# Attention loop with merges ahead of maxima, spread gate values, an earlier output weight and a moved transposition

## The reference, cut to what matters

```
mod = silu(c) @ wmod;  ga = sign(ga) * max(|ga|, 0.25)
h = layernorm(x) * (1 + ca) + sa
x = x + ga * (softmax(mask(q k^T / 4)) v) @ wo          # block 0, attention
h = layernorm(x) * (1 + cb) + sb
gate = softmax over the 16 best of 64 experts
x = x + gb * ((h @ A.T) * gate) @ B.T * 2               # block 0, mixture
w1 = (Wq + Wk + Wv + low rank parts) / 3                # block 1, decoded from 4-bit codes
```

## Time and profile before

| | us |
|---|---|
| median of 3 runs | 947.92 |
| lowest, highest | 945.81, 948.16 |
| profiled execution, its own time | 945.97 |
| span of its instructions | 944.2 |
| PE busy | 861.7 (91%) |
| DVE busy | 681.2 (72%) |
| ACT busy | 533.1 (56%) |
| POOL busy | 191.1 (20%) |
| mean granted TensorE clock | 0.974 of 2.4 GHz |

### The profile page before, as it was taken

The page is one execution under the profiler, slowest core; times in us unless marked ns, Lnnn a source line. Parts: engine busy times, 40 slices in busy tenths (PEclk is TensorE's granted clock), DMA queues, the critical chain, the costliest instruction groups (busy, mean ns, idle before and its releaser), DMA issues.

```text
span 944.2 us, 13669 instructions
## 1 busy us (share of the span) xinstructions
PE 861.7 (91%) x5096; PEld 679.8 (72%) x5096; DVE 681.2 (72%) x1066; ACT 533.1 (56%) x707; POOL 191.1 (20%) x199
## 2 busy tenths in 40 slices
PE   3799899998859699998999999999988999999996
PEld 1466666666637587786888888788876888888885
DVE  3845777888769677688777778577787866667842
ACT  3412576667652525476566667477727766666830
POOL 3002565677637114200000000000040000000004
PEclk9798899999989999999999999999989999999999
DMA  8587378878534112115233333143312433332202
GB/s 297 177 254 158 35 99 130 126 91 129 89 90 167 34 45 73 51 33 161 81 107 110 105 96 89 46 111 90 114 43 68 115 107 90 110 92 67 67 1 90
DMA packets 38450, 95.35 MB, mean 101 GB/s; under 512 B 7144, under 2 KB 10216, under 8 KB 37360
## 3 DMA queue, kind: packets, MB, share of 16 engines
q1 hardware_dynamic: 34256, 89.11, 38.9%
q10 hardware_dynamic: 4128, 5.36, 1.7%
HBM read 79.56 MB, written 2.21 MB: 87 GB/s over the span
## 4 chain that ended last, share of the span: by engine, by line
PE 59%; DVE 6%; issue 2%; ACT 2%; POOL 1%; DMA 1%; SPq 0%; POOLq 0%; DVEq 0%; ACTq 0%
PE PS L1602 13%; PE PS L1603 13%; PE PS L1604 13%; PE PS L1913 5%; PE PS L1912 5%; PE PS L1911 5%; POOL X L776 1%; DVE ACC L1224 1%; PE PS L1894 1%; DVE SCR L1209 1%; PE PS L1882 1%; PE PS L1646 1%; DVE ST L1151 1%; DMA WOF<-in_WO 1%; PE PS L1841 1%
## 5 line engine op out<-in xcount | busy, mean ns | idle before, releaser
L899 ACT ACTIVATE PL<-CODE 128x1024 f32<-128x1024 int32 x200 | 202.5, 1057 | 58.8 <-DVE ACC L1224 56.1
L1602 PE MATMUL PS<-HH,WRH 128*128 128x512 f32 x448 | 177.0, 395 | 9.8 <-DVE WRL L1236 4.4
L1603 PE MATMUL PS<-HH,WRL 128*128 128x512 f32 x448 | 176.3, 393 | 0.0
L1604 PE MATMUL PS<-HL,WRH 128*128 128x512 f32 x448 | 176.0, 393 | 0.0
L776 POOL TENSOR_TENSOR X<-X,SCR 128x512 f32<-128x512 f32 x32 | 42.5, 1339 | 560.7 <-DVE SCR L1209 560.6
L1224 DVE SCALAR_TENSOR_TENSOR ACC<-PL,ACC 128x1024 f32<-128x1024 f32 x100 | 122.8, 1228 | 8.4
L947 ACT ACTIVATE PT<-PS 128x512 f32<-128x512 f32 x160 | 85.4, 601 | 57.9 <-PE PS L1720 38.5
L793 POOL TENSOR_TENSOR QS<-ident,MX 64x256 fp32r<-64x256 f32 x128 | 97.2, 759 | 71.9 <-DVE MX L1381 51.6
L1602 PEld LDWEIGHTS PS<-HH,WRH 128*128 128x128 f32 x448 | 85.2, 190 | 29.8 <-issue 5.4
L1604 PEld LDWEIGHTS PS<-HL,WRH 128*128 128x128 f32 x448 | 85.2, 190 | 17.9
L1603 PEld LDWEIGHTS PS<-HH,WRL 128*128 128x128 f32 x448 | 85.1, 190 | 17.2
(11 more groups left out here) (230 smaller groups left out, 1525.2 us busy)
## 6 DMA issues: line engine op xcount, KB each, us to landing
CODE<-in_CODES SPq DMA_DIRECT2D x50, 512.0 KB, 3.5
SCALE<-in_SCALES SPq DMA_DIRECT2D x100, 256.0 KB, 4.0
WM<-in_WM SPq DMA_DIRECT2D x12, 1024.0 KB, 5.3
QS<-FQ SPq DMA_DIRECT2D x32, 256.0 KB, 5.2
X<-in_X ACTq DMA_DIRECT2D x2, 1024.0 KB, 12.7
KS<-KHL SPq DMA_DIRECT2D x32, 64.0 KB, 5.3
KN<-KHL SPq DMA_DIRECT2D x32, 64.0 KB, 4.2
GAB<-gates SPq DMA_DIRECT2D x4, 512.0 KB, 3.7
```

What stands on the lines that cost most here:

```text
L899: nc.scalar.activation(PL[:, n % 3], CODE[:, p % 2], ACT.Prelu, scale=scale, bias=bias, alpha=alpha).then_inc(s_plane, 1)
L1602: nc.tensor.matmul(dst, lh, rh, start=start and k == 0, stop=False)
L1603: nc.tensor.matmul(dst, ll, rh, start=False, stop=False)
L1604: ins = nc.tensor.matmul(dst, lh, rl, start=False, stop=stop and k == KC - 1)
```

## The change

- `step_at` loses its shift by one slot: every decoding step is one slot earlier, and the last fold lies in the loop, behind unit 62's exponentials on ACT. Three entries of `CODES_AT` and `SCALES_AT` move one stack ahead to match it.
- `add_odd_values` stands ahead of the maxima of unit 12, 20, ..., 60, and `add_odd_sums` behind the maxima of the same unit.
- The four operations of the gate values lie behind units 2, 5, 6 and 10. SP stores the gates at stack 6, not 3.
- SP waits for the last curve (`s_plane`), not for the last sum, ahead of the load of `WOF`. ACT rounds `WOF` after the exponentials of unit 63.
- `a1` is transposed after the sixth output product, and DVE copies it ahead of the seventh gated output.

```
-CODES_AT = {0: (0, 1), 4: (2,), 6: (3,), 9: (4,), 12: (5,)}
-SCALES_AT = {0: (0, 1), 6: (2,), 9: (3,), 13: (4,), 15: (5,)}
+CODES_AT = {0: (0, 1), 4: (2,), 6: (3,), 9: (4,), 11: (5,)}
+SCALES_AT = {0: (0, 1), 6: (2,), 8: (3,), 12: (4,), 15: (5,)}
+A1_AT = 5
+GATE_AT = [2, 5, 6, 10]
 def step_at(n):
-    at = n // 8 * len(slots) + slots.index(n % 8) - 1
-    return divmod(at, STEPS) if at >= 0 else None
+    return divmod(n // 8 * len(slots) + slots.index(n % 8), STEPS)
...
     # job_list
     for t in range(NT):
         jobs.append((("wo", t), 0))
-    jobs.append((("a1",), 0))
+        if t == A1_AT:
+            jobs.append((("a1",), 0))
...
     # SP
-                if n == STACKS:
+                if n == 2 * STACKS:
                     sp.wait_ge(s_mr, 1)
...
-            sp.wait_ge(s_used, len(CAPS) * N_QKV)
+            sp.wait_ge(s_plane, len(CURVES) * N_QKV)
             for h in range(REP):
                 sp.dma_start(WOF[32 * h:32 * h + 32], ...
+            sp.wait_ge(s_used, len(CAPS) * N_QKV)
             sp.wait_ge(s_wf, N_QKV - 1)
             sp.dma_start(ATF[:], ...
...
     # ACT
-                if n == units - 2:
+                if n == units - 1:
                     act.wait_ge(s_wo, 16 * REP)
+                    act.wait_ge(s_used, len(CAPS) * N_QKV)
                     nc.scalar.activation(WOH[:], WOF[:], ACT.Copy).then_inc(s_w0h, 1)
-            fold(N_QKV - 1)
             act.wait_ge(s_pv, units)
...
     # DVE; gate_value(step) is gate_values() cut in its four operations
             for n in range(B * GROUPS * TB):
+                if pair_at(n, 4) is not None:
+                    add_odd_values(pair_at(n, 4))
                 for pair in range(2):
                     ...
-                if n == TB - 1:
-                    gate_values()
+                if n in GATE_AT:
+                    gate_value(GATE_AT.index(n))
                 if pair_at(n, 4) is not None:
-                    add_odd_values(pair_at(n, 4))
-                if pair_at(n, 5) is not None:
-                    add_odd_sums(pair_at(n, 5))
+                    add_odd_sums(pair_at(n, 4))
...
                     t = b * TB + ti
+                    if t == A1_AT:
+                        halve(A1, ("a1",))
                     if t + 1 < NT:
                         gated(("wo", t + 1))
...
                 if b:
-                    halve(A1, ("a1",))
                     modulate(1, b - 1)
...
     # PE: the four transpositions of a1 stand behind wo product 5, not behind product 7
```

More of the change, by code:

```diff
@@ L1140, in mod_column, with gate_value @@
                     nc.vector.tensor_scalar(MCOL[:, l, v], MCOL[:, l, v], 1.0, None, ALU.add).then_inc(s_mc, 1)
[L1142 to L1148, removed]
+            def gate_value(step):
+                if step == 0:
+                    dve.wait_ge(s_free, J["gsum",] + 1)
+                    link(nc.vector.tensor_scalar(MR[:], GR[:], 0.0, 2.0, ALU.is_ge, ALU.mult))
+                elif step == 1:
+                    link(nc.vector.scalar_tensor_tensor(GR[:], GR[:], -1.0, GR[:], ALU.mult, ALU.max))
+                elif step == 2:
+                    link(nc.vector.tensor_scalar(GR[:], GR[:], 0.25, None, ALU.max))
+                else:
+                    nc.vector.scalar_tensor_tensor(MR[:], MR[:], -1.0, GR[:], ALU.add, ALU.mult).then_inc(s_mr, 1)
             def stats(t):
@@ L1760, in _ @@
                         ).then_inc(s_mm, 1)
[L1761 to L1765, removed]
+                if t == A1_AT:
+                    dst = begin(("a1",))
+                    pe.wait_ge(s_lq, 16)
+                    for k in range(KC):
+                        ins = nc.tensor.transpose(dst[:, k * P:(k + 1) * P], LQF[:, k * P:(k + 1) * P], ident[:])
+                    ins.then_inc(s_mm, 1)
             norm(1, 0)
```

## The result

The changed kernel takes 932.7 us (median of 4 runs, 931.15 to 934.63) beside 947.5 us for the kernel before in the same comparison (945.81 to 948.16): ratio 0.9848, 95% interval 0.9824 to 0.9871. The profiled execution of after takes 933.26 us (span 931.5), 12.7 less than that of before.

A forecast was written before the change was run, and what follows sets the result against it. The attention loop was bound by PE and DVE waiting on each other, the stretch behind it by a chain through DMA, ACT and DVE. Gains 3.7 + 6.2 + 0.3 + 3.2 = 13.4 us off 947.92 gave 934.5, range 929.5 to 940.0.

The forecast's parts named there:

- gate values: Loop's start: PE's 3.42 us idle before unit 4 and the half clock behind it go, 3.7 us gained.
- merges, with the steps that move: Attention loop: seven 1.3 us waits for `DEN` go, less the value additions' price, with shifted decoding steps: 6.2 us gained.
- output weight: End of attention: load wait goes, but `ATL` holds DVE's splits instead of the division; 0.3 us gained.
- transposition: Between `norm(1, 0)` and `w1`: PE's 3.19 us wait for `A1` goes, 3.2 us gained.
- The upper bound of 4.2: Gate values at the loop's start: gain of 4.2 us if the gate operations are all hidden.
- the text's own list: Signs of error: waits of scores for maxima growing by 0.7 us at seven units, or half clock between 285 and 320.
- Rival (b): Merges: DVE becomes the bound at every merge, gain 1.9 instead of 6.2 us, 938.8 us in all; chance 0.14.
- Rival (a): End of attention: splits get in before `ATL`, gain 3.8 instead of 0.3 us, 931.0 in all; chance 0.2.
- The rest of the kernel: From 331 us on, PE busy 592 of 613 us: untouched, should keep its length and only start earlier.
- the half clock between 285 and 320: Sign of error: half clock between 285 and 320 us would show the forecast wrong.
- rival (d): Output products to `w1`: idle stretches bring clock falls, slower than before, about 951 us with 33 us half clock; chance 0.03.

The follow-up runs named there:

- the splits apart: Kernel before with the merges moved and the splits of heads moved from units 51 and 59 to 53 and 61: 938.68 us, ratio 0.9918.
- the last kernel: Changed kernel with splits of heads moved, `ATL` behind second norm, `WOH` before unit 63's exponentials, last fold behind loop, two splits ahead of `WOL`: 924.64 us.
- the changed kernel's second profile: The changed kernel run once more, nothing edited, as base for three variants of it: 932.3 us, ratio 0.9845.
- `ATL` in quarters: Changed kernel with POOL's `ATL` cut in four instructions of a quarter at the same place: 931.23 us, ratio 0.9831.
- the early splits: Changed kernel with the three splits of heads moved ahead of the output weight's subtraction on DVE: 930.11 us, ratio 0.9821.
- late `ATL`: Changed kernel with POOL's `ATL` moved behind the second norm, ahead of the router: 931.6 us, ratio 0.9831.

## Why the prediction was right, step by step

| step | predicted gain | in the traces | alone, by the medians |
|---|---|---|---|
| gate values | 3.7 | 4.6 (alone 5.0) | 5.0 |
| merges, with the steps that move | 6.2 | 6.8 | 3.1; 5.7 with the splits apart |
| output weight | 0.3 | 1.0 | 1.6, with what it gives in the loop |
| transposition | 3.2 | 3.3 | 4.1 |
| sum | 13.4 | 15.7 less 3.0 elsewhere | 14.8 for the whole |

*Gate values: right in mechanism, low in size.* Unit 4's maxima came 2.6 us earlier relative to the first ones, against 2.5. The term that was too small is the clock's: I gave 1.3 us for units 4 and 5 at full rate, and it is 2.0 in the whole change and with the gates alone, where unit 4 came 3.0 us earlier by itself. The row was there: PE is busy 5.13 us at half clock in the earlier trace rows, at most 2.6 us of lost work, and I took half of it. The upper bound of 4.2 was too low as well.

*Merges: right, with one cost unseen.* The waits for `DEN` went, and the loop from unit 6 to 62 is 6.8 us shorter against 6.2. Cycle by cycle of eight units it is 0.6, 1.2, 0.6, 0.6, 0.5, 2.3 and 1.1, where the sum had 0.6, 1.2, 0.65, 0.65, 0.6, 1.8 and 0.65. In the last of them 0.7 us come from the shifted steps, between units 58 and 59 (the output weight alone has them too); the sum did not have these. By the text's own list it would be wrong if the waits for maxima grew by 0.7 us at seven units; in after one grew by 0.65 (unit 60, 0.97 to 1.62) and four new ones are 0.6 each ((4.0 - 1.62) / 4), the 0.67 that the sum had charged there. Rival (b) needed that price a second time at each merge and did not come. What I left out is that the wait behind a slot with three operations can be followed by a fall, 1.6 us each time it is. The forecast was kept from most of this by luck, by a shift of steps that it had priced for another reason: at unit 51 no curve sum stands any more, so the changed kernel has one such slot and the merges alone have two.

*Output weight: right order, small term.* `WOL` ended 13.6 us behind the maxima of unit 63, against 13.8, and `ATL` got in. The splits ended 6.2 us behind `WOL`, not 6.5. From there to the fifth product it took 7.9 us as worked out. That is 27.7 us, where the forecast's terms give 28.2. Rival (a), the splits ahead of `ATL`, did not come, and its price of 3.8 us was too high. It let the first four products run in 10.9 us; with `ATL` away altogether they took 12.6, at half clock for 3.4 us behind 4.89 us of idle time, and the stage gained 1.2 us. In after PE stood 1.06 us before the fifth product, not 3.4, for the same reason.

*Transposition: right.* 3.3 against 3.2. Its 4.1 by the medians may hold a part of the 1.6 us that a fall ahead of `w1` costs; that is not shown.

*The rest of the kernel* was forecast to keep its length. In the profile it lost 2.5 us (3.2 less 0.7), to falls behind waits that both kernels have; the first of them is the half clock between 285 and 320 that the text named as a sign of error. It is not rival (d): the products from 285.4 to 298.7 us ran at 1.00. But it is the cost that (d) was about, half clock behind PE's waits, at a place where the forecast had put nothing: it came in five of the eight executions with the moved transposition and in none of the other six, and the 1.6 us behind the wait ahead of `w1`, which the change takes away, came in four of those six. The forecast had neither term.

*The sum: near, in part by luck.* The four steps gave 2.3 us more than forecast in the traces, and 3.0 us went elsewhere, so 12.7 against 13.4 is two misses that nearly cancel. The medians gain 14.4 to 14.8 us. That they gain more than the two profiles fits with before's profile, which lacks the fall ahead of `w1`, and after's, which lost 3.2 us behind the router; the executions that were not profiled can't show it.

## What to carry to other kernels

A wait taken off an engine is paid by whatever now shares a slot with the moved operation: count how many operations stand in a row between two answers to TensorE, and spread them, since the longest gap can cost twice, once as idle time and once as clock. When a transfer comes off the chain, follow the chain to the next pair of engines that share a port before pricing it: 5.6 us of DMA were worth 1.0 us here, 2.2 with `ATL` moved away too, and 6.2 in the last kernel, where PE's first products no longer start behind an idle stretch. Before the difference of two profiles is put down to the edit or to chance, cut every profile at the same events and see in which stage it lies: a fall at the same microsecond in two kernels need not stand behind the same wait.

## What the runs showed of the hardware

- **A wait of 1.62 us can be followed by half clock, in a loop where PE is otherwise about 94% busy.** (160.99 of 171.9 us in after.) Seven such waits were profiled: four were followed by 1.2 GHz for 3.4 us (both with the merges alone, one in the changed kernel's second profile, one with `ATL` in quarters), three were not (after, the early splits, late `ATL`). Waits of 0.97, 1.3 and 0.60 us in the same loop, from unit 6 on, brought none. I can't say from these runs what decides between the two outcomes; the changed kernel gave both from one program, so it is nothing in the order of its instructions.
- **The half clock came in lengths of 3.4, 6.8 or 10.2 us** behind the same idle stretch: at the end of attention 6.8 in before and 10.2 with the gates alone; 3.4 in the first profile of after and 6.8 in the second. There the longer ones cost nothing, since DVE is the bound: the stage took 28.6 us in both of the first pair and 27.6 in both of the second.
- **What did set profiles apart in stages that no edit had touched**: the start of the loop (first maxima between 83.6 and 87.2 us in the fourteen), 1.6 us of a fall in the loop, 1.6 us behind the wait ahead of `w1`, and 1.3 to 3.2 us behind the router's waits. So the medians were needed to size each part.
- **DVE and POOL took turns at SBUF, one operation each, while both had work waiting**, in both directions: POOL between two operations of DVE (after, and the kernel with quarters, three times in a row), DVE between two of POOL (the early splits).
